# Attention over key blocks: chunk by chunk over all head groups, with all keys kept on chip

## What is computed

```python
xn = _layernorm(x, axis=-1)
qkv = x @ Wqkv.T                       # attention, on xn
q = q * cos + rotate_half(q) * sin
k = k * cos + rotate_half(k) * sin
scores = jnp.einsum('bhqd,bhkd->bhqk', q, k) * scale
scores = jnp.where(causal[None, None], -jnp.inf, scores)
attn = jax.nn.softmax(scores, axis=-1)
out = jnp.einsum('bhqk,bhkd->bhqd', attn, v)
...
g = jnp.einsum('td,eid->tei', xf, w11)  # experts, on xn
u = jnp.einsum('td,eid->tei', xf, w33)
act = jax.nn.silu(g) * u
y = jnp.einsum('tei,te,edi->td', act, c, w22)
shared = jax.nn.silu(xf @ sw1.T) * (xf @ sw3.T) @ sw2.T
...
x = x + attention(xn) + experts(xn)
```

## Time and profile before

| | us |
|---|---|
| median of 3 runs | 907.65 (906.76 to 915.72) |
| profiled execution | 914.75 |
| its span, first to last instruction | 913.0 |
| TensorE busy in the span | 836.4 |
| VectorE busy | 605.6 |
| ScalarE busy | 497.1 |
| GpSimd busy | 505.1 |

### The profile page before, as it was taken

One profiled execution on the slowest core, in us unless ns is written; L12 is line 12 of the kernel. 1 busy time (PEld: TensorE's weight loads), 2 busy tenths in 40 slices (PEclk: granted clock), 3 DMA queues, 4 the chain that ended last, 5 costly groups with the idle time before them and its releaser, 6 DMA issues.

```text
span 913.0 us, 17558 instructions
## 1 busy us (share of the span) xinstructions
PE 836.4 (92%) x5281; PEld 455.5 (50%) x5282; DVE 605.6 (66%) x1179; ACT 497.1 (54%) x1214; POOL 505.1 (55%) x651
## 2 busy tenths in 40 slices
PE   5799977698989998989999999998999999999997
PEld 2466644233343433368888887773343343433444
DVE  2677776888876686755555555555788777888322
ACT  3556523155556655635444544456676756667672
POOL 3566640499989302046666666626878888810000
PEclk9999987799999999999999999999999999999999
DMA  7025554610000212037777777774585555510011
GB/s 222 1 78 175 172 175 138 165 32 19 1 19 1 67 44 64 1 102 229 234 234 227 225 244 229 140 140 71 74 170 87 72 90 72 88 18 1 13 35 47
DMA packets 81986, 96.15 MB, mean 105 GB/s; under 512 B 13030, under 2 KB 73446, under 8 KB 81894
## 3 DMA queue, kind: packets, MB, share of 16 engines
q0 software_dynamic: 19968, 31.47, 19.1%
q1 hardware_dynamic: 45033, 46.80, 17.3%
q10 hardware_dynamic: 16896, 16.78, 5.4%
HBM read 61.11 MB, written 33.82 MB: 104 GB/s over the span
## 4 chain that ended last, share of the span: by engine, by line
PE 68%; issue 14%; DVE 10%; SPq 2%; ACT 2%; DVEq 1%; DMA 1%; POOLq 1%; POOL 1%; ACTq 0%
PE bank L1190 13%; PE bank L1173 13%; PE vector_banks L1149 11%; PE vector_banks L1268 7%; DVE mpart L955 7%; PE vector_banks L1041 5%; PE vector_banks L1062 4%; PE bank L1281 3%; PE bank L1062 3%; PE bank L1041 2%; PE vector_banks L1210 2%; PE bank L1078 2%; PE bank L1176 1%; PE vector_banks L1152 1%; ACT probs L710 1%
## 5 line engine op out<-in xcount | busy, mean ns | idle before, releaser
L955 DVE TENSOR_REDUCE mpart<-vector_banks 128x2 f32<-128x1024 f32 (+3 forms) x320 | 330.7, 1062 | 100.8 <-PE vector_banks L1149 58.2
L710 ACT ACTIVATE probs<-bank 128x512 f32<-128x512 f32 (+3 forms) x428 | 213.5, 537 | 136.7 <-PE bank L1176 64.7
L1173 PE MATMUL bank<-turned 99*128 99x512 bf16 (+3 forms) x640 | 207.2, 355 | 17.4 <-ACT probs L710 5.3
L587 POOL DMA_INDIRECT turned<-normed_rows,tok_i x128 | 125.6, 981 | 138.6 <-PE vector_banks L1041 85.1
L1149 PE MATMUL vector_banks<-turned 96*128 96x512 bf16 (+3 forms) x640 | 185.3, 360 | 12.8 <-DVE mpart L955 12.2
L602 POOL DMA_INDIRECT res<-expert_rows,slot_i x96 | 148.9, 1551 | 43.3 <-issue 28.6
L1173 PEld LDWEIGHTS bank<-turned 99*128 99x128 bf16 x640 | 58.9, 97 | 186.2 <-ACT probs L710 86.6
L710 ACT ACTIVATE at_first<-bank 128x512 f32<-128x512 f32 (+3 forms) x212 | 106.2, 532 | 74.4 <-PE bank L1176 35.6
L1268 PE MATMUL vector_banks<-xn_all,probs 128*128 x512 | 136.3, 389 | 3.0 <-issue 1.3
L1190 PE MATMUL bank<-probs,V 128*32 128x512 f32 (+3 forms) x856 | 102.2, 549 | 0.0
L1268 PEld LDWEIGHTS vector_banks<-xn_all,probs 128*128 128x128 f32 x512 | 87.8, 191 | 16.0 <-issue 7.7
(11 more groups left out here) (152 smaller groups left out, 967.8 us busy)
## 6 DMA issues: line engine op xcount, KB each, us to landing
expert_rows<-probs ACTq DMA_DIRECT2D x32, 512.0 KB
term_rows<-at_first SPq DMA_DIRECT2D x96, 128.0 KB
turned<-term_rows SPq DMA_DIRECT2D x32, 384.0 KB, 5.0
xn_all<-wexp SPq DMA_DIRECT2D x32, 384.0 KB
normed_rows<-xn_all SPq DMA_DIRECT2D x4, 512.0 KB, 5.5
turned<-normed_rows,tok_i POOLq DMA_INDIRECT x128
out<-res SPq DMA_DIRECT2D x16, 128.0 KB, 1.7
res<-x SPq DMA_DIRECT2D x1, 1536.0 KB, 9.2
```

The costliest lines, as they stand in the source:

```text
L587: gp.indirect_dma_start(xg[:, n % XR, :], None, xn_dram, bass.IndirectOffsetOnAxis(ap=tok_i[:, n:n + 1], axis=0)).then_inc(rows_in[n % XR] ...
L710: A(PT[v // 2 % 6][:, v % 2, 0:width], bank[A_BANK[step][0]][:, 0:width], ACT.Exp).then_inc(s["scalar_bank_read"], 1)
L955: V.tensor_reduce(mpart[:, t % TPC, 2 * j:2 * j + 2, p], ring[:, :, 0:w], AX.X, ALU.max).then_inc(s["vector_bank_read"], 1)
L1173: last = mm(ring[:, 0:CH - off], k_turned(parity(g), slice(0, KM), h, kb * P, P), q_turned(slice(0, KM), h, c * CH + off, CH - off), start ...
```

## The change

The key blocks run chunk by chunk over all head groups: (0,0), (1,0), (2,0), (3,0), (0,1) and so on. The experts stand ahead of (2,2), after 72 key blocks in place of 64. Each chunk's strips are due six steps ahead of its first score, and the tokens are spread up to key block 64 in place of 50.

All keys stay on chip (`keys`, by chunk and group); queries have a ring of four slots (`Q_SLOTS`), and a slot is loaded again when the chunk four places ahead has had its last score. The rows of ones under the keys are copied once for each chunk. Values lie in `V` with 17 columns a head (16 and a one); a head's weights are 32 columns that reach into the next head's, and these rows of the result are not read. `take_v`, `V4` and the semaphores `v4_ready`, `ones_made` are gone. Working buffers of the first stages have moved to other places.

```diff
-TOKENS_FROM, TOKENS_TO = 8, 50
-EXPERTS_AT = (1, NCH - 1)
+TOKENS_FROM, TOKENS_TO = 8, 64
+EXPERTS_AT = (2, NCH - 2)
+V1 = DH + 1
+VROW = (H - 1) * V1 + VW + 1
+Q_SLOTS = 4
...
-    key_blocks = [(g, c, kb) for g in range(NG) for c in range(NCH) for kb in range(TPC * (c + 1))]
-    for c in range(1, NCH):
-        scores += strips(0, c)
-        score_goals.append((4 * (key_blocks.index((0, c, 0)) - 1), len(scores)))
-    score_goals[-1] = (4 * (key_blocks.index((0, NCH - 1, 0)) - 1), len(scores))
-    for g in range(1, NG):
-        for c in range(NCH):
-            scores += strips(g, c)
-        score_goals.append((4 * (key_blocks.index((g, NCH - 1, 0)) - 2), len(scores)))
+    key_blocks = [(g, c, kb) for c in range(NCH) for g in range(NG) for kb in range(TPC * (c + 1))]
+    for c in range(NCH):
+        for g in range(NG):
+            if c or g:
+                scores += strips(g, c)
+                if c == 0 or g in (0, NG - 1):
+                    score_goals.append((4 * key_blocks.index((g, c, 0)) - 6, len(scores)))
...
+        def q_slot(rows, g, c):
+            at = chunk_at(g, c) % Q_SLOTS * HG * CH
+            return QB[rows, at:at + HG * CH]
+        def k_turned(rows, g, j, k0, w):
+            at = (chunk_at(g, k0 // CH) * HG + j) * CH + k0 % CH
+            return KB[rows, at:at + w]
...
# SyncE, quarter by quarter
-                sp.wait_ge(s["terms_stored"], 16 * STORES * (quarter + 1))
-                for kind in range(2):
-                    load_terms(kind, 0, quarter)
+                if quarter == 0:
+                    sp.wait_ge(s["terms_stored"], 16 * STORES)
+                    for g in range(NG):
+                        load_keys(g, 0)
+                        load_queries(g, 0)
...
+            sp.wait_ge(s["terms_stored"], 16 * STORES * 4)
+            for c in (1, 2):
+                for g in range(NG):
+                    load_keys(g, c)
+                set_ones(c)
+                if c == 1:
+                    store_weights(3)
+            def next_queries(some):
+                for i in some:
+                    used(*chunks[i - Q_SLOTS])
+                    load_queries(*chunks[i])
+            sp.wait_ge(s["plan_ready"], 1)
+            next_queries([Q_SLOTS])
+            for g in range(NG):
+                load_keys(g, NCH - 1)
+            set_ones(NCH - 1)
...
# ScalarE
-                copy(v_all[:, bass.ds(t, 1), :].rearrange("p a n -> p (a n)"), bank[3 + b][:, 0:D])
+                copy(V[:, t, 0:H * V1].rearrange("p (h v) -> p h v", v=V1)[:, :, 0:DH],
+                     bank[3 + b][:, 0:D].rearrange("p (h d) -> p h d", d=DH))
-            take_v(0)
...
# TensorE
-                            last = mm(pv_bank[VW * h:VW * (h + 1), off:CH], V4[:, kb, h, :],
+                            last = mm(pv_bank[VW * h:VW * (h + 1), off:CH], V[:, kb, (HG * g + h) * V1:(HG * g + h) * V1 + VW],
```

More of the change, by code:

```diff
@@ L160, in whole_order @@
                 values(block)
-            order.append(later.pop()[1])
+            order += [step for _, step in later]
+            later.clear()
             pending = []
@@ L257, in carve @@
             return take
-        turned = sb("turned", [P, 2 * HG * T])
+        KW = NG * HG * CH // 2
+        keys = sb("keys", [P, NCH * KW])
+        queries = sb("queries", [P, Q_SLOTS * HG * CH // 2])
         probs = sb("probs", [P, 4 * 2 * CH])
-        QW = HG * T // 2
-        EARLY_WORDS = 15360
-        first_words = sb("at_first", [P, EARLY_WORDS])
-        at_first = carve(first_words, EARLY_WORDS)
-        before = carve(turned[:, 2 * QW:3 * QW], QW)
-        routing = at_first
-        counting = carve(turned[:, 3 * QW:], QW)
-        ffn = carve(turned[:, 3 * QW:], QW)
+        o_words = sb("o_words", [P, NT * D])
+        more_words = sb("more_words", [P, 3840])
+        spare = sb("spare", [P, 3456])
+        at_first = carve(o_words, NT * D)
+        staging = [carve(keys[:, c * KW:(c + 1) * KW], KW) for c in (2, 1)]
+        routing = carve(keys[:, 3 * KW:], KW)
+        before = carve(more_words, 3840)
+        counting = carve(spare, 3456)
+        ffn = carve(spare, 3456)
         before_probs = carve(probs, 4 * 2 * CH)
@@ L683, in _ @@
                     terms_turned(t, kind)
-            def take_v(group):
-                copy(V4[:, :, :, 0:DH], v_all[:, :, group * GW:(group + 1) * GW].rearrange("p t (h d) -> p t h d", d=DH)
-                     ).then_inc(s["v4_ready"], 1)
             def attend(steps, pvs, score_steps):
```

242 lines of the change are left out of this document (111 added, 131 removed).

## The result

The changed kernel takes 913.7 us, the median of its runs, against 907.65 us: a ratio of 1.0056 with a 95% interval of 1.0038 to 1.0073. (The ratios are not quite the quotients of the two medians; they differ from them by up to 0.2%.) That is within 1% and inside the range, but on the other side of no change than the 903 us of the forecast. One run in fifteen took 2815 us; it and the few far-off runs of later batches are not in the ratios. Timed again beside other kernels it took 913.8 us, ratio 1.0068 (1.0041 to 1.0096). The profiled execution took 913.14 us (span 911.2), close to its own median, where that of before stood 7 us above its own.

The account below looks back on a forecast made before the run. TensorE, busy for 92% of the span, was to set the time through its order and gaps. Chunk prices summed to 908.2 us against a profiled span of 913.0; carried over to the 907.65 median, 903 us, range 893 to 915.

Parts of the forecast that it names:

- The anchor: Whole kernel: sum of 908.2 us from one profiled execution of 914.75, its 7 us over the median carried over, giving 903.
- moved strips: Strips shifted between chunks cost 0.43 us each; (3,2), with 31 strips for 24, was given 37.8 us.
- The gather: (1,2), where the gathers now start: VectorE's 2.83 us stall comes again and carries 3.0 us, making 36.4.
- The front: (0,0): 11 strips remain of 19, so 9.6 us come off, leaving 26.0 us, bounds 22 to 33.
- rival B: Front falls to 22 us, narrow chunks' turnings hide, the gathers' stall does not return: 893 to 898 us; chance 0.20.
- The narrow chunks: (1,0), (2,0) and (3,0): 13.1, 15.0 and 17.9 us, together 46.0, bounds 40 to 63.
- E: Chunk boundaries: two steps are too few to hide the copy, twelve at 1.0 us each, 915 us; chance 0.03.
- Rival D: (1,0), (2,0) and (3,0) lose TensorE's clock, 17 us if all fall, 8 to 9 if half: 912 to 920; chance 0.13.
- Two banks: Tokens step moves from step 190 to 243; two banks cost 0.25 us a block; (0,1) to (2,1) take 80.1 us.
- The restart: (2,2), behind the experts: 1.4 us added for restarting, within 35.4 us for the chunk.
- Behind the experts: From the experts to the end: near 275 us, 295 now, called the firmest part.

Follow-up runs that it names:

- the second profile: Kernel before, unchanged, run again: 908.46 us, ratio 0.9982, span 906.4; for the front and chunk 2, the changed kernel, unchanged, run again: 914.18 us.
- the third: Changed kernel, unchanged, timed again beside the even-strips versions on one chip: 913.8 us, ratio 1.0068 to the kernel before.
- the experiment: Changed kernel with TOKENS_TO 50 in place of 64, so the third bank joins earlier: 908.06 us, ratio 0.9985 to the kernel before.
- even strips: Changed kernel without own strip goals for (3,1) and (3,2), TOKENS_TO 64: 902.2 us, ratio 0.9886; again 901.79 us, 0.9943, to the kernel before.
- the last batch: One chip, against the kernel before: changed kernel 913.8 us, even strips with TOKENS_TO 64 901.79 us, even strips with 50 905.04 us.
- the version that turns earlier: Changed kernel with strips from (2,0) on, but for (3,3), due 22 steps ahead in place of 6: 910.03 us, ratio 1.0005 to the kernel before.

## Why the prediction was right and wrong

Two steps failed. The anchor made a gain of 4 to 5 us out of a sum that, from a usual execution, comes to no change. The price of moved strips is what turned no change into the loss that was measured; with one line that spreads the strips the loss is gone, and 0.6% under the kernel before is reached. The other steps came out or matter less.

**The anchor, wrong.** The sum was made from one execution, and its distance of 7 us to the median was then taken off the result. But 5.5 of these 7 us lay in (1,0) and (1,1) of the kernel before, and the sum had no term in which they came along, save 3.0 for the gathers: (1,0) and (1,1) of the changed kernel were priced by the rows of group 2. They were taken off twice. With the second profile as the base (span 906.4), the same sum without the 3.0 for the stall says a span of 905.2: 1.2 us less, no change that can be measured. The measured 911.2 is still 6.0 above that. The text even said that the median lay 7 us lower "although its parts are what I price", and did not ask which part was too long. The rows had it: (1,0) and (1,1) took 43.5 us against 34.5 for (2,0) and (2,1), of which two banks (2) and three token steps (1) explain 3.

**The gather, wrong.** The 2.83 us of VectorE were taken for something that comes with the gathers. (1,2) took 32.7 us and not 36.4: nothing came.

**The front, right, with some luck.** 26.2 us for 26.0, and 26.2 in the second profile; but 22.3 in the third, in the same order, at a granted clock of 0.85 in place of 0.70:

```profile
143.80:166.10 22.30, 16.54 (x142) 9.30 (x143) 15.29 (x53) 6.41 (x15) 3.83 (x6) 0.85 0.60 184
```

That is the 22 us of rival B; the sum could name only one of the two. VectorE's reductions are 7.4 us in the first profile (10 of them) for the 8.2 worked out for eleven:

```profile
141.50:167.70 26.20, 7.42 (x10) 0.70 0.69 194
```

**The narrow chunks, right.** 13.0, 15.5 and 18.0 us for 13.1, 15.0 and 17.9. VectorE is busy for 16.4 of the last. TensorE waits for no query load in any profile of the changed kernel, nor, which was E's sign, for VectorE's copy of the maxima, for which it waited 3.0 us before. Rival D has no part in these chunks: the clock is 0.98 to 1.00 from 167.7 to 214.2.

**Two banks, near.** (0,1) to (2,1) took 81.3 for 80.1. Taken alone, the price was 0.25 us a block and the experiment gives 0.17 once the token steps are taken off. The `tokens` step's block had no term, 1.7 us. (3,1) took 32.0 for 33.4, and holds 22 strips by the order, not the 24 of the working.

**Moved strips, wrong.** The largest miss: (2,2) and (3,2) took 82.9 us and were given 73.2 (the second and third profile have 80.1 and 83.5). A strip was priced at 0.43 us, its matmuls, and the wait behind it at nothing. That does not hold where three stand in a block and VectorE is late. With 31 strips (3,2) took 43.4 us, or 42.1 in the profile without a half-clock interval in it; with even strips it has 25 and took 36.9. Of the 5.6 us above the forecast of 37.8, the interval is 1.3. Between 42.1 and 36.9 lie six strips, 2.6 us at the price, and 2.6 that the price does not have: TensorE waits 3.7 us for VectorE's reductions in the one and 1.9 in the other, and VectorE is busy for 36.6 of the 42.1 us. The last 1.7 are there with even strips too, whose 25 strips would be 35.2 by the price. In (2,2) the density matters little (39.1 with even strips): its first two blocks took 7.1 us for 4.6 in the (2,2) of before, the last two 7.8 for 6.5, with a turning in both cases and five strips for four, and one block had half clock, 4.50 for 3.21. The restart was given 1.4 us and cost 2.4.

**Behind the experts.** "The firmest part", 275 us, was 282.6, because of these two chunks: chunk 3 came near the forecast, 45.8 to 47.1 us a chunk and 59.6 for the end.

**The clock.** D's mechanism was there, at another place and for another reason. The Trainium skill, "TensorE: Matmul & The Clock Gate", section "A second HAM failure mode: psum-queue depth-cycling", lays an oscillating clock in one kernel to the pauses between groups of matmuls that cycle through PSUM. The trace agrees as far as a pause goes: the clock fell at the block of (2,1) where TensorE had waited 1.5 and 0.7 us for VectorE, and stayed at 1.00 there once the strips were even, with the scores on two banks both times. It does not make the pause enough, as the turning of (0,1) shows.

Against the kernel before the clock explains a part at most. At 0.974 the changed kernel took 912.1 to 913.3 us in the first batch, and the kernel before 906 to 907 in the second and 906 to 910 in the third; in the last batch, where several runs of both were timed on one chip, at 0.977, it is 910.4 to 910.7 against 904.2 to 908.2. But the usual clock there is 0.972 for the changed kernel and 0.9755 for the kernel before, so that some of the 5.7 us between the medians comes with it.

**Where the 5 us went.** Against the second profile of before, span 906.4: (0,0) gives 8.6 us and chunk 3 14.1; (1,0) to (3,0) cost 11.8, chunk 1 6.3, chunk 2 9.1, and the experts' stretch with the start 0.4. The gain is in chunk 3 and the front, the cost in the rest of chunk 0 and in chunks 1 and 2. Some of it is work that only changed place: chunk 1 has ten token steps for three, 2.4 us. (The other two profiles of the changed kernel give 6.3 and 9.6 for chunk 2.) Each chunk's turning now stands in a last, narrow block. From (0,1) to (1,3) such a block takes 4.6 to 5.5 us, and 6.8 to 7.5 with an interval in it; it takes 2.0 to 2.8 us, once 3.4, in the version that turns earlier, where a full block takes about 2.0 more for the turning.

**Open.** What held VectorE and ScalarE in the first profile of before. Why the third bank, worth 2 us in (0,2), is worth nothing in sum once the strips are even. And what else than a wait decides whether the clock falls.

## What to carry to other kernels

Before parts are priced from a profiled execution, ask how far it stands from the median and find the part in which that lies; a distance may be carried over only if what makes it is also in the new sum. Work that is "only moved" keeps its price while the engine behind it keeps up: look at what stands per narrow block, not per stretch, and spread fills over the whole distance to their due date. And see what a short wait of TensorE costs after it has ended: here 2.2 us of waiting were followed by 3.4 us of half clock in all three profiles.

## What was not expected of the hardware

Many of the granted clock's intervals fall at the same blocks in execution after execution (the last of (2,1), at 289 to 294 us, in all three profiles of the changed kernel; the last of (3,2), at 705 to 708 us, in two). So a waiting place often marks itself in one profile, but it takes two to tell it from a single event: the interval in (2,0), at 193 us, is in one profile and in none of the three of the changed kernel, with the same order there. And time follows the mean granted clock within one kernel, though not to the microsecond: 910.4 us at 0.977, 913.8 and 915.6 at 0.972, and 918.9 at 0.966 on one chip.
